# Where the queries' projection stands in the odd rounds of an attention pipeline

## What is computed

```python
q = (x @ Wq + bq).reshape(bs, n_ctx, HEADS, d)
kv = (data @ Wkv + bkv).reshape(bs, n_data, HEADS, 2 * d)
scores = jnp.einsum('bqhd,bkhd->bhqk', q, k) * scale
attn = jax.nn.softmax(scores, axis=-1)
out = jnp.einsum('bhqk,bkhd->bqhd', attn, v).reshape(bs, n_ctx, WIDTH)
return out @ Wp + bp
...
logits = xf @ router_w
scores, idx = jax.lax.top_k(logits, K)
gate = jax.nn.softmax(scores, axis=-1)
...
x = x + _L0_xattn_ref(_layernorm(x, axis=-1), ctx_1024, ...)
x = x + _L0_ffn_ref(_layernorm(x, axis=-1), ...)
```

## Time and profile before

| | us |
|---|---|
| median of 3 runs | 931.85 |
| the three runs | 931.54, 931.85, 938.29 |
| the profiled execution | 938.24 |
| its span | 936.4 |
| PE busy | 887.6 (95%) |
| DVE busy | 745.0 (80%) |
| ACT busy | 646.3 (69%) |
| POOL busy | 408.9 (44%) |

### The profile page before, as it was taken

How to read it: one execution, slowest core, us unless ns; L and a number is a source line. 1 busy time by engine, 2 the same in 40 slices (tenths; PEclk the granted TensorE clock), 3 DMA queues, 4 the chain that set the end, 5 groups by cost and what they waited for, 6 DMA issues and landing times.

```text
span 936.4 us, 19131 instructions
## 1 busy us (share of the span) xinstructions
PE 887.6 (95%) x6174; PEld 795.6 (85%) x6174; DVE 745.0 (80%) x1757; ACT 646.3 (69%) x1297; POOL 408.9 (44%) x649
## 2 busy tenths in 40 slices
PE   4999999999998998999999999999999999999995
PEld 3888878887877876788999989899898998998994
DVE  2688888888878888787979788887877877778783
ACT  3676766767666774775977777867776776777773
POOL 3456576777776575330432240605114234052052
PEclk8899999999999999999999999999999999999998
DMA  6332333342255337643756455827817838466442
GB/s 144 66 67 49 74 85 69 86 99 61 63 128 177 114 118 268 182 112 121 217 121 185 135 155 168 240 94 186 278 45 215 282 68 259 177 178 177 147 79 27
DMA packets 132368, 129.17 MB, mean 138 GB/s; under 512 B 59936, under 2 KB 117152, under 8 KB 132128
## 3 DMA queue, kind: packets, MB, share of 16 engines
q1 hardware_dynamic: 119392, 110.36, 38.7%
q0 software_dynamic: 12864, 17.44, 10.3%
HBM read 102.01 MB, written 25.36 MB: 136 GB/s over the span
## 4 chain that ended last, share of the span: by engine, by line
PE 78%; DVE 11%; issue 3%; ACT 3%; another core or an unknown queue 1%; POOL 1%; SPq 1%; DMA 0%; POOLq 0%; DVEq 0%; ACTq 0%
PE bank L1985 35%; PE bank L2029 18%; PE bank L1820 5%; PE bank L1737 4%; PE bank L1977 3%; PE bank L1755 3%; PE bank L1774 2%; DVE maxes L1238 2%; PE bank L1784 2%; PE bank L2017 1%; PE bank L1954 1%; DVE probs L1244 1%; DVE q_l L1279 1%; PE bank L1792 1%
## 5 line engine op out<-in xcount | busy, mean ns | idle before, releaser
L852 POOL DMA_INDIRECT out_rows<-yo,token x68 | 114.4, 1682 | 384.9 <-ACT yo L1095 319.8
L1985 PE MATMUL bank<-xh,wh 128*128 128x512 f32 (+1 forms) x672 | 234.7, 349 | 5.4 <-DVE gate_in L1610 4.8
L1985 PE MATMUL bank<-xl,wh 128*128 128x512 f32 (+1 forms) x672 | 228.9, 341 | 0.0
L1985 PE MATMUL bank<-xh,wl 128*128 128x512 f32 (+1 forms) x672 | 228.5, 340 | 0.0
L1586 DVE TENSOR_TENSOR wl<-raw,wh 128x1024 fp32r<-128x1024 f32 x126 | 152.4, 1220 | 13.0 <-ACT wh L1026 12.1
L1985 PEld LDWEIGHTS bank<-xh,wh 128*128 128x128 f32 x672 | 127.9, 190 | 20.1 <-DVE gate_in L1610 7.5
L2029 PE MATMUL bank<-wh,hh 128*128 128x256 f32 x496 | 141.9, 286 | 1.7 <-issue 1.3
L1985 PEld LDWEIGHTS bank<-xh,wl 128*128 128x128 f32 x672 | 127.8, 190 | 14.9
L2029 PE MATMUL bank<-wh,hl 128*128 128x256 f32 x496 | 140.4, 283 | 0.0
L2029 PE MATMUL bank<-wl,hh 128*128 128x256 f32 x496 | 140.4, 283 | 0.0
L1985 PEld LDWEIGHTS bank<-xl,wh 128*128 128x128 f32 x672 | 128.2, 191 | 10.8
(11 more groups left out here) (195 smaller groups left out, 1861.6 us busy)
## 6 DMA issues: line engine op xcount, KB each, us to landing
raw<-in_W SPq DMA_DIRECT2D x42, 1024.0 KB
raw<-in_Wo SPq DMA_DIRECT2D x25, 1024.0 KB
whole<-in_W SPq DMA_DIRECT2D x8, 1024.0 KB, 7.6
xs<-in_x SPq DMA_DIRECT2D x32, 128.0 KB, 2.7
out_rows<-x SPq DMA_DIRECT2D x32, 128.0 KB, 1.8
shared<-z_rows SPq DMA_DIRECT2D x7, 520.0 KB
bo_row<-in_bo SPq DMA_DIRECT2D x25, 128.0 KB
k_blocks<-k_parts SPq DMA_DIRECT2D x128, 19.2 KB
```

The source lines that it names most:

```text
L852: e.indirect_dma_start(out=out, out_offset=bass.IndirectOffsetOnAxis(ap=token[j % 4][:, s:s + 1], axis=0), in_=yo[j % 2][:, s, :], in_offs ...
L1985: mm = e.matmul(ps[:, h * cols:(h + 1) * cols], ws[split_before(j) % 2][:, w, c, m * P:(m + 1) * P], xx[j % 2][:, c, 0:cols], start=(h == ...
```

## The change

In odd rounds from 1 on, PE's `queries` leaves its place ahead of `scores(i, 1)` and stands behind `project(i - 2)`, directly ahead of `values(i - 1)`. The list in `misc_turns` moves it in the same way, so the turns of the two banks change in odd rounds. On ACT the q_t copies and q_h move from ahead of `make_y` to behind `logits_copy`, ahead of `make_z`. On DVE q_l moves behind x1 and the statistics, ahead of `normalized`; `x_sums` and `x_variance` of odd rounds move ahead of `make_x1`. Batch 0's queries (round −1) stay where they were.

```diff
         uses += [("v", nb)] if batch and even else []
-        uses += [("q", nb)] if batch and not even else []
         uses += [("logits", i - 5)] if 0 <= i - 5 < NT else []
         uses += [("proj", i - 2)] if 0 <= i - 2 < NT else []
+        uses += [("q", nb)] if batch and not even else []
...
                 if 0 <= i < NT:
                     exp_scores(i, 0)
-                if batch and not even:
+                if i < 0 and batch and not even:
                     queries(nb)
...
                 if 0 <= i - 5 < NT:
                     logits_copy(i - 5)
+                if 0 < nb < BATCH and not even:
+                    queries(nb)
+                if 0 <= i - 5 < NT:
                     make_z(i - 5)
...
-                if batch and not even:
-                    low_queries(nb)
+                if nb == 0 and not even:
+                    low_queries(0)
+                if not even and 0 <= i + 5 < NT:
+                    x_sums(i + 5)
+                    x_variance(i + 5)
                 if 0 <= i - 2 < NT:
                     make_x1(i - 2)
...
                 if 0 <= i - 2 < NT:
                     x1_sums(i - 2)
-                if 0 <= i + 5 < NT:
+                if even and 0 <= i + 5 < NT:
                     x_sums(i + 5)
                 if 0 <= i - 2 < NT:
                     x1_variance(i - 2)
-                if 0 <= i + 5 < NT:
+                if even and 0 <= i + 5 < NT:
                     x_variance(i + 5)
+                if 0 < nb < BATCH and not even:
+                    low_queries(nb)
                 if 0 <= i - 1 < NT:
                     normalized(i - 1)
...
-                if batch and not even:
+                if i < 0 and batch and not even:
                     queries(nb)
...
                 if 0 <= i - 2 < NT:
                     project(i - 2)
+                if i % 2 and 0 < i // 2 + 1 < BATCH:
+                    queries(i // 2 + 1)
```

## The result

The changed kernel takes 943.32 us (median of 6 runs, 941.83 to 946.00), and the kernel before, on the same chip, 932.69 (median of 6, 931.54 to 938.29). The ratio is 1.0108, with a 95% interval of 1.0084 to 1.0132: slower by 1.1%, +10.6 us. The forecast was 945. One run further down (945.54, with queries ahead of the projection) was in a slower state of the core and is left out.

What follows compares the result with a forecast made beforehand. TensorE, busy 95%, was taken as the bound. Ten steady pairs +4.9, rounds 1 to 5 +2.1, rounds 27 and 29 +0.2: +7.2 us, 938.24 becomes 945.4; main case 941 to 950, range up to 955.

Steps and rivals of the forecast that it cites:

- The queries' start: Odd rounds, TensorE: queries wait some 0.6 us for ScalarE's logits copy to release their bank, starting at +5.25.
- The chain: From queries' end through q_t, q_h, q_l to next scores 2.66 us, covered only by values' 2.28; odd round 1.26 longer.
- The first half of an even round: Even rounds, first to second scores: 3.45 us without keys (taken as 3.7), 4.25 with keys, where 5.11 stood.
- The sum of ten pairs: Second scores of round 6 to those of round 26: 179.41 us before, 183.0 or 184.3 after, taken as +4.9.
- Rounds 1 to 5: Rounds before the routing work is complete: +1.1 us in round 5, +0.5 each in 1 and 3, together 2.1.
- Rounds 27 and 29: Held by VectorE's tables and its share of the first weights; reordering only exchanges work in one queue, +0.2 us for both.
- The profiled execution and the median: Late signals in odd rounds put the profiled 938.24 us 6.4 above the median; changed kernel still 945, +13 on the median.
- (a): Rival: late signals also hit the queries' own signal in odd rounds 13 to 27, +8 us, 953; chance 0.13.
- (b): Rival: the summed difference stays, but the quiet state helps both kernels alike, 939 us; chance 0.20.
- (c): Rival: q_l takes 1.2 us in every moved round, beside GpSimd, 949 us; chance 0.12.
- (d): Rival: not slower, VectorE's relief in even first halves outweighs the chain; 935 us by trace, 928 by median; chance 0.08.
- (e): Rival: nothing happens, since queries wait where they waited, 932 us; chance 0.02.

Runs made afterwards that it cites:

- the doubled copy: One more ScalarE copy of q_t ahead of q_h: in the changed kernel 950.96 us, ratio to before 1.0162; in the kernel before 934.19, ratio 1.0012.
- the second profile: The kernel before, unchanged, profiled once more: this execution took 932.41 us, with no wait put down to an unknown queue in round 17.
- The kernel with the busy round 27: The changed kernel with 14 small bf16 matmuls on TensorE ahead of the second scores of round 27: 939.75 us, ratio to the kernel before 1.0070.

## Why the prediction was right, step by step

**The first half of an odd round** was to last 2.39; it lasts 2.38 in round 17 and 2.51 in round 15. Right.

**The queries' start** was to be +5.25 behind a wait for the logits copy; it is +5.27 and +5.29. Right in place and releaser, and within 0.04 in time, and the experiment with the logits copy in front showed that this wait, and not an arrival of PE, set the start.

**The chain** was put at 2.66 from the queries' end to the scores, and the round at 9.81. From 154.71 and 1.89 of matmul to 159.02 are 2.42, and rounds of 9.6. The mis-sized term is q_l: I took its mean of 0.93, it takes 0.69 in eleven of the fifteen moved rounds (0.70 to 0.87 in the other four). That the chain is on the path, and that nothing but the values covers it, is shown by the doubled copy.

**The first half of an even round** was to be 3.45, taken as 3.7, without keys and 4.25 with them. From round 8 to 24 it is 3.60 in three rounds and 3.79 and 3.95 in two, 3.71 in the mean, and 4.25. Right.

**The sum of ten pairs** was +4.9 by the trace of before; it is +2.5 against that trace and +5.6 against the one without late signals (181.94 against 176.32). The 2.4 too much are nearly all the ten q_l terms: 9.81 less 9.60, ten times, 2.1.

**Rounds 1 to 5** were put at +2.1 and cost +2.5 (the second scores of round 6 at 72.31, against 69.80) or +2.6 (against 69.72). The sum is right by luck. Round 5 cost 0.75 and not 1.1, round 3 cost 0.2, which round 4 gave back, and round 1 cost 1.3 against the second profile and 1.8 against the first, in a stretch (20 to 33 us) whose granted clock is 0.54 here and 0.87 and 0.66 there. The kernel with the busy round 27, the same program up to there, reached this point 1.0 later still, at 73.28.

**Rounds 27 and 29** were put at +0.2. From the second scores of round 26 to those of round 31 are 47.89, and 48.01 in the trace that the prediction was made from, but 46.15 in the kernel before without late signals: +1.7. Against its own trace the number holds only because round 29 had been long there from late signals (10.37). This step failed. Against the quiet execution round 27 is 2.1 longer (11.81 against 9.73) and round 29 1.4 (10.24 against 8.86), and rounds 28 and 30 give back 0.8 and 0.9. "The reordering only exchanges work in one queue" is true of a queue that has slack behind it; here x1 and its statistics came between the tables and q_l, and PE waited for it. The side remark, that idle gaps of 0.4 to 0.7 cost no clock, is not touched: the gap here was 1.30, and the fall of the clock behind it cost at most 0.6.

These three add up to 2.6 + 5.6 + 1.7 = 9.9 at the second scores of round 31 (302.14 against 292.19), of a median difference of 10.6. Behind them the traces have 637.9 us in the changed kernel and 638.4, 639.2 and 640.3 in the three profiles of the kernel before, so that the loss lies in the rounds, as far as a spread of 2 us lets one tell.

**The profiled execution and the median.** The forecast rested on a reading that could have been wrong: that the trace of before was 6.4 above its median because of late signals, and that the changed kernel has nothing to win where they are absent. The first half was borne out: the quiet execution of before is 5.0 shorter up to round 31, no late signal stands in the trace after, and the loss was 10.6 by the medians but 3.6 by the two first profiles. How the time was lost was described for 1.9 of the 5.0 only. How the changed kernel would do with late signals no run shows. That the forecast of 945 came within 1.7 is in part luck: on the trace that it was summed from, the loss up to round 31 was 4.9 and not 7.2, and the profiled execution of the changed kernel was the shortest of its six, 1.5 below their median.

**The rivals.** (a) Late signals at the queries' own semaphore: the profile after has none. (b) The sum of 7.2 on the median: it was 10.6, outside. (c) q_l at 1.2: wrong in direction, it runs at 0.69. In five of the fifteen rounds no GpSimd instruction runs beside it, and in round 15 it starts at 158.28, ahead of GpSimd's spreading of values at 158.48, and it is that one which takes 2.12 instead of the 1.77 of the earlier trace rows. In the kernel with queries ahead of the projection the order is the other: GpSimd's xf starts at 152.67, q_l at 152.90, and q_l takes 1.07 while that xf keeps its 0.74.

```profile
152.67 0.74 POOL L742 TENSOR_TENSOR xf<-y,rows 128x256 f32<-128x256 f32 x1
...
152.90 1.07 DVE L1282 TENSOR_TENSOR q_l<-q_t,q_h 128x512 fp32r<-128x512 f32 x1
```

The Trainium skill, page SBUF — State Buffer, section "Who interferes with whom", has the rule that two such instructions contend and the first to issue keeps the port; the trace agrees with it in these two places. It also corrects my reading of round 17: q_l (169.59) started ahead of xf (170.21), so xf is the later one there, and what made q_l 1.25 long may be GpSimd's indirect DMA instruction, which ran from 169.22 to 170.19. That is a reading of times and is not shown; in round 15 of the same trace such an instruction (151.63 to 152.60) ran beside q_l and q_l took 0.66. (d) needed odd rounds of 9.32 or less, by pairs of 17.94; the execution of before without late signals has pairs of 17.63 (176.32 over ten), which puts that point at 9.01. Odd rounds of 9.6 are past either. The experiment with the logits copy in front had 8.8 to 9.2 and still was 1.0024 of before, since its even first halves were 4.26 and not the mean of 3.98 that the point assumes. (e) did not occur.

What stays open: what makes signals of PE's matmuls reach ACT and VectorE up to 1.6 us late in some executions (only that they came together with the longer time is seen, in one profile), and the 3.0 us (3.6 less 0.6) by which the medians of the changed kernel and of its variant with a busy round 27 differ beyond what their profiles show.

## What to carry to other kernels

When a producer is moved in an in-order queue, count the distance to its consumer first: the chain of the other engines behind it, less the work of the waiting engine that still lies between. Look also at who held the buffer before it at its new place: here a bank released late cost 0.6 us a round, a chain of 2.4 us under values of 2.3 cost 0.2, and one call more between producer and consumer (0.95) took away both in the steady rounds. Look for the rounds that are not steady, too: where VectorE built tables, work put ahead of q_l was waited for in full. Give the queue that you relieve no credit before you have seen what it does with the time: VectorE's routing work was the better thing to move, and it could be moved without touching the queries. And before two profiles are subtracted, ask of each how far its own time is from its kernel's median.

## What the runs showed of the hardware that was not expected

- Signals of TensorE's matmuls that arrive late: in one of three profiles of the same program ACT copies logits at +8.09 of round 17 instead of +6.48, and 5.0 us of the run's time go with it. One profile shows it; the cause is open.
- When a VectorE and a GpSimd instruction overlap, the longer time fell to the one that started later: q_l 0.69 and then the spreading 2.12 (1.77 before); xf 0.74 and then q_l 1.07; q_l and then xf 1.21 (0.73 elsewhere).
- A gap of 1.30 us was followed by a granted clock of 0.61 over 4.4 us in round 27, while gaps of 1.34 and 1.42 in two profiles of the kernel before were not: the length of one gap does not tell. The clock's fall cost at most 0.6 us of that round and 0.14 us over rounds 26 to 31, since VectorE was waited for behind it.
